# Order of the start-up and of the slots in a fused lightning-attention and mixture-of-experts kernel: x ahead of the decay rates, 12 of 16 decay tables and half of Wo in slot 0, counts behind the next q projection

## What is computed

```python
xn = layernorm(x)
# branch 1: lightning attention, 16 heads of 32, chunks of 128 tokens
q, k, v = silu(xn @ Wq), silu(xn @ Wk), silu(xn @ Wv)
D[c, s] = exp(ld * (c - s)) * (c >= s)                 # one table per head
o_intra = ((q @ k.T) * D) @ v
o_inter = (q @ S) * exp(ld * (c + 1))
S_new   = exp(ld * 128) * S + (k * exp(ld * (127 - s))).T @ v
gate    = (xn @ Wg1) @ Wg2
o       = rmsnorm_per_head(o * sigmoid(gate)) * norm_w
attn    = o @ Wo
# branch 2: 8 experts, top 2 of 8, capacity 1280 tokens per expert
moe     = sum over the kept top-2 of  p * (relu(xn @ w1[e]) @ w2[e])
out     = x + attn + moe
```

## Time and profile before

| | us |
|---|---|
| median of 3 runs | 2138.87 (2136.01 to 2139.21) |
| the profiled execution | 2135.27 |
| its span, first to last instruction | 2133.5 |
| PE busy | 2061.2 (97%) |
| DVE busy | 826.1 (39%) |
| ACT busy | 549.3 (26%) |
| POOL busy | 481.7 (23%) |
| mean granted TensorE clock | 0.991 of full speed |

### The profile page before, as it was taken

The page is one execution under the profiler, slowest core; times in us unless marked ns, Lnnn a source line. Parts: engine busy times, 40 slices in busy tenths (PEclk is TensorE's granted clock), DMA queues, the critical chain, the costliest instruction groups (busy, mean ns, idle before and its releaser), DMA issues.

```text
span 2133.5 us, 27452 instructions
## 1 busy us (share of the span) xinstructions
PE 2061.2 (97%) x11288; PEld 1691.5 (79%) x11288; DVE 826.1 (39%) x1582; ACT 549.3 (26%) x985; POOL 481.7 (23%) x371
## 2 busy tenths in 40 slices
PE   5899999999989999999999999999999999999997
PEld 3677787778778888888888888888888888888886
DVE  4666676667563123223312422321242124223211
ACT  4223222332232123212312312321231123123211
POOL 2544454435430202021120211102020102111011
PEclk9899999999999999999999999999999999999999
DMA  4320212012142214133321512422151215124021
GB/s 145 88 81 21 81 61 81 27 65 91 42 141 88 41 45 117 58 70 73 116 45 45 161 29 63 116 61 40 50 141 31 47 40 163 27 65 114 20 31 20
DMA packets 83961, 151.34 MB, mean 71 GB/s; under 512 B 16768, under 2 KB 16768, under 8 KB 83824
## 3 DMA queue, kind: packets, MB, share of 16 engines
q1 hardware_dynamic: 63424, 105.65, 14.9%
q0 software_dynamic: 20400, 43.74, 11.3%
HBM read 109.82 MB, written 39.53 MB: 70 GB/s over the span
## 4 chain that ended last, share of the span: by engine, by line
PE 88%; DVE 5%; DMA 2%; issue 2%; ACT 1%; POOL 1%; another core or an unknown queue 1%; SPq 0%; POOLq 0%; DVEq 0%; ACTq 0%
PE bank L1092 45%; PE bank L1359 32%; PE bank L1099 2%; PE bank L1215 2%; PE bank L1399 2%; PE bank L1182 1%; DVE xnT_lo L810 1%; PE bank L1141 1%; PE bank L1204 1%; PE bank L1198 1%; DVE turned L913 0%; DVE gated L911 0%; DVE stats L793 0%; ACT oT_hi L676 0%
## 5 line engine op out<-in xcount | busy, mean ns | idle before, releaser
L1044 DVE SCALAR_TENSOR_TENSOR h_lo<-bank,h_hi 128x512 fp32r<-128x512 f32 x256 | 176.9, 691 | 788.9 <-ACT h_hi L750 781.9
L1092 PE MATMUL bank<-xT_hi,w_hi 128*128 128x512 f32 x1024 | 406.6, 397 | 1.1 <-issue 1.0
L1359 PE MATMUL bank<-w_hi,h_hi 128*128 128x512 f32 x1024 | 398.6, 389 | 1.6 <-DVE h_lo L1044 1.6
L1092 PE MATMUL bank<-xT_hi,w_lo 128*128 128x512 f32 x1024 | 399.5, 390 | 0.0
L1359 PE MATMUL bank<-w_hi,h_lo 128*128 128x512 f32 x1024 | 398.7, 389 | 0.0
L1092 PE MATMUL bank<-xT_lo,w_hi 128*128 128x512 f32 x1024 | 398.5, 389 | 0.0
L1359 PE MATMUL bank<-w_lo,h_hi 128*128 128x512 f32 x1024 | 398.4, 389 | 0.0
L750 ACT ACTIVATE h_hi<-bank 128x512 fp32r<-128x512 f32 x256 | 153.1, 598 | 820.0 <-PE bank L1092 806.8
L577 POOL DMA_INDIRECT out_rows<-y,add_row x80 | 128.2, 1603 | 777.5 <-ACT y L743 706.7
L1359 PEld LDWEIGHTS bank<-w_hi,h_hi 128*128 128x128 f32 x1024 | 192.2, 188 | 42.4 <-DVE h_lo L1044 2.5
L1092 PEld LDWEIGHTS bank<-xT_hi,w_lo 128*128 128x128 f32 x1024 | 192.2, 188 | 41.7
(11 more groups left out here) (185 smaller groups left out, 2382.8 us busy)
## 6 DMA issues: line engine op xcount, KB each, us to landing
raw_weights<-in_L_ffn_w SPq DMA_DIRECT2D x256, 256.0 KB, 4.2
x_in<-in_L_attn_x SPq DMA_DIRECT2D x32, 256.0 KB, 3.1
xn_rows<-xn SPq DMA_DIRECT2D x32, 256.0 KB, 2.4
x_res<-in_L_attn_x SPq DMA_DIRECT2D x32, 256.0 KB, 4.4
out_rows<-y_attn SPq DMA_DIRECT2D x32, 256.0 KB
out_rows<-y,add_row POOLq DMA_INDIRECT x80, 6.0
gathered<-xn_rows,gather_row POOLq DMA_INDIRECT x76, 3.5
attn_raw<-in_L_attn_Wq SPq DMA_DIRECT2D x4, 256.0 KB, 8.0
```

Source lines behind the costliest of these rows:

```text
L1044: v_.scalar_tensor_tensor(h_lo[f % 2][:, 0:n * P], h_bank[f % 2][:, 0:n * P], 0.0, h_hi[f % 2][:, 0:n * P].bitcast(F32), ALU.max, ALU.subt ...
L1092: last = mm(dest, at(left[l], t), at_r(right[r], t), start=(i == 0), stop=(i == n - 1))
L1359: last = mm(y_bank[i][:, :], hx[f % 2][:, part], wx[c][:, f % FPC, :], start=(f == 0 and l == 0), stop=(f == FT - 1 and l == 2))
```

## The change

- SP loads tiles 0 to 3 of x first. The decay rates are started from ACT's own queue, as the first thing that ACT does.
- ACT makes 4 of the 16 decay tables at the start (those of unit 0) and 12 in slot 0, between tanh(0) and silu of q(1). The small high parts are made ahead of silu of q(0). The high part of Wo moves behind silu of k(1). In every unit the squares of unit u-1 are made right behind tanh(u), where those of unit u stood at the unit's end, and oT_hi(u-1) stands ahead of the four `xnT_high` in the third unit.
- POOL masks 4 tables at the start and 12 at the head of slot 0; `norm_scale(2)` moves from ahead of the slot table's initialisation to behind the 8 routes of slot 0.
- DVE makes `diff` ahead of the first `norm_pair`. The low part of Wo, `norm_pair(2)` and `normalise` of tiles 4 and 5 move from ahead of `choose(0)` into slot 0, behind `gate_output(0)`. In every unit all four masks go together, mean square of u-1 follows, then the states, `give_slots`, `scale_heads(u-1)` and oT_lo(u-1), and only then, in the third unit, the four xnT_lo. In a first unit one `add_residual` goes ahead of `norm_pair`.
- PE turns the router logits between v tiles 0 and 1, where it did so behind v tile 3, and counts behind the q projection of the next unit, where it did so behind `score`. At the end `project_out(2)` is split, and its third part waits for oT_lo behind `turn_first(3)`.

```diff
@@ -337,12 +337,4 @@
 
-            load_x(0)
-            load_x(1)
-            sp.dma_start(ld_row[:, :], log_decay.partition_broadcast(P)).then_inc(S["decays_loaded"], 16)
-            ld_groups = log_decay.rearrange("(g h) -> h g", h=HPG)
-            for h in range(HPG):
-                sp.dma_start(ld_col[h * HD:(h + 1) * HD, :],
-                             ld_groups[h, :].partition_broadcast(HD),
-                             allow_slow_non_contiguous=True).then_inc(S["decays_loaded"], 16)
-            load_x(2)
-            load_x(3)
+            for t in range(TPG):
+                load_x(t)
             for u in range(UNITS):
@@ -487,9 +479,12 @@
 
-            pool.wait_ge(S["tables_made"], HEADS)
-            g_.affine_select(out=intra_decay[:, :, :], in_=intra_decay[:, :, :],
-                             compare_op=ALU.is_ge, fill=0.0, base=0, pattern=[[0, HEADS], [1, P]],
-                             channel_multiplier=-1).then_inc(S["tables_masked"], 1)
+            def mask_tables(first, behind):
+
+                pool.wait_ge(S["tables_made"], behind)
+                g_.affine_select(out=intra_decay[:, first:behind, :], in_=intra_decay[:, first:behind, :],
+                                 compare_op=ALU.is_ge, fill=0.0, base=0, pattern=[[0, behind - first], [1, P]],
+                                 channel_multiplier=-1).then_inc(S["tables_masked"], 1)
+
+            mask_tables(0, HPG)
             decayed_k(0)
             decayed_q(0)
-            norm_scale(2)
 
@@ -539,2 +534,4 @@
                     head_scales(u - 1)
+                else:
+                    mask_tables(HPG, HEADS)
                 if i == 0:
@@ -550,2 +547,4 @@
                             route(g, t, r)
+                    if g == 0:
+                        norm_scale(2)
                     if g < SUPERS - 1:
@@ -612,2 +611,8 @@
             a = nc.scalar
+            act.dma_start(ld_row[:, :], log_decay.partition_broadcast(P)).then_inc(S["decays_loaded"], 16)
+            ld_groups = log_decay.rearrange("(g h) -> h g", h=HPG)
+            for h in range(HPG):
+                act.dma_start(ld_col[h * HD:(h + 1) * HD, :],
+                              ld_groups[h, :].partition_broadcast(HD),
+                              allow_slow_non_contiguous=True).then_inc(S["decays_loaded"], 16)
             act.wait_ge(S["decays_loaded"], 16 * (1 + HPG))
@@ -618,5 +623,9 @@
             a.activation(chunk_decay[:, :], ld_col[:, :], ACT.Exp, scale=float(P)).then_inc(S["decay_made"], 1)
-            act.wait_ge(S["diff_ready"], 1)
-            for h in range(HEADS):
-                a.activation(intra_decay[:, h, :], diff[:, :], ACT.Exp, scale=ld_row[:, h:h + 1]).then_inc(S["tables_made"], 1)
+
+            def decay_tables(heads):
+                act.wait_ge(S["diff_ready"], 1)
+                for h in heads:
+                    a.activation(intra_decay[:, h, :], diff[:, :], ACT.Exp, scale=ld_row[:, h:h + 1]).then_inc(S["tables_made"], 1)
+
+            decay_tables(range(HPG))
 
@@ -685,3 +694,2 @@
             weights_high("k")
-            silu_q(0)
             act.wait_ge(S["small_loaded"], 16 * 7)
@@ -689,2 +697,3 @@
             a.copy(g2_hi[:, :], g2_raw[:, :]).then_inc(S["small_hi"], 1)
+            silu_q(0)
             silu_k(0)
@@ -694,3 +703,2 @@
                 silu_v(t)
-            weights_high("o")
 
@@ -708,2 +716,6 @@
                 a.activation(tanh_g[:, :], proj[1][:, :], ACT.Tanh, scale=0.5).then_inc(S["tanh_ready"], 1)
+                if u > 0:
+                    square(u - 1)
+                if u == 0:
+                    decay_tables(range(HPG, HEADS))
                 if u < ATTN_UNITS - 1:
@@ -711,2 +723,6 @@
                     silu_k(u + 1)
+                if u == 0:
+                    weights_high("o")
+                if u > 0:
+                    oT_high(u - 1)
                 if i == 2 and g < SUPERS - 1:
@@ -714,6 +730,2 @@
                         xnT_high(TPG * (g + 1) + j)
-                if u > 0:
-                    oT_high(u - 1)
-                if u < ATTN_UNITS - 1:
-                    square(u)
                 if i == GROUPS - 1 and g < SUPERS - 1:
@@ -833,3 +845,3 @@
                 dve.wait_ge(S["scored"], u + 1)
-                dve.wait_ge(S["tables_masked"], 1)
+                dve.wait_ge(S["tables_masked"], 1 if u == 0 else 2)
                 for r in rs:
@@ -948,4 +960,2 @@
 
-            norm_pair(0)
-            norm_pair(1)
             dve.wait_ge(S["consts_made"], 3)
@@ -953,2 +963,4 @@
             v_.memset(taken[:, :], 0.0).then_inc(S["carry_zero"], 1)
+            norm_pair(0)
+            norm_pair(1)
             for t in range(TPG):
@@ -973,6 +985,2 @@
             gate_low(0)
-            weights_low("o")
-            norm_pair(2)
-            normalise(TPG)
-            normalise(TPG + 1)
 
@@ -983,8 +991,8 @@
                 g, i = u // GROUPS, u % GROUPS
-                mask(u, (0, 1))
-                if i == 0:
-                    read_counts(g)
+                mask(u, range(HPG))
                 if u > 0:
                     mean_square(u - 1)
-                mask(u, (2, 3))
+                if i == 0:
+                    read_counts(g)
+                states(u)
                 if i == 0:
@@ -995,6 +1003,2 @@
                         v_.tensor_scalar(spare_used[:, 1, :], taken[0:1, :], float(MAIN + P), None, ALU.is_gt).then_inc(S["spare_known"], 1)
-                states(u)
-                if i == 2 and g < SUPERS - 1:
-                    for j in range(TPG):
-                        xnT_low(TPG * (g + 1) + j)
                 if u > 0:
@@ -1002,8 +1006,19 @@
                     oT_low(u - 1)
+                if i == 2 and g < SUPERS - 1:
+                    for j in range(TPG):
+                        xnT_low(TPG * (g + 1) + j)
                 gate_output(u)
+                if u == 0:
+                    weights_low("o")
+                    norm_pair(2)
                 if i == 0:
+                    if g > 0:
+                        add_residual(TPG * (g - 1), proj[0])
                     if g < SUPERS - 1:
                         norm_pair(2 * (g + 1) + 1)
+                    if g == 0:
+                        normalise(TPG)
+                        normalise(TPG + 1)
                     if g > 0:
-                        for j in range(TPG):
+                        for j in range(1, TPG):
                             add_residual(TPG * (g - 1) + j, proj[j % 2])
@@ -1243,3 +1258,3 @@
             pe.wait_ge(S["g1_lo_made"], 1)
-            pe.wait_ge(S["logits_copied"], 1)
+            turn_logits(0)
             project_v(1)
@@ -1250,3 +1265,2 @@
             pe.wait_ge(S["consts_made"], 12)
-            turn_logits(0)
 
@@ -1255,4 +1269,2 @@
                 score(u)
-                if i == 0:
-                    count(g)
                 turn_kd(u)
@@ -1270,2 +1282,4 @@
                 project("q", u + 1, proj[0], "q_projected")
+                if i == 0:
+                    count(g)
                 update_states(u)
@@ -1294,3 +1308,3 @@
                     pe.wait_ge(S["g1_lo_made"], g + 2)
-                    pe.wait_ge(S["logits_copied"], g + 2)
+                    turn_logits(g + 1)
                     project_v(TPG * (g + 1) + 1)
@@ -1300,3 +1314,2 @@
                     project_v(TPG * (g + 1) + 3)
-                    turn_logits(g + 1)
 
@@ -1314,8 +1327,8 @@
             turn_first(1)
-            pe.wait_ge(S["oT_lo_made"], u)
-            project_out(2, last_out_bank[2], (0, 1, 2), True, False)
+            project_out(2, last_out_bank[2], (0, 1), True, False)
             turn_first(2)
             turn_first(3)
-            project_out(0, last_out_bank[0], (2,), False, False)
-            project_out(1, last_out_bank[1], (2,), False, False)
+            pe.wait_ge(S["oT_lo_made"], u)
+            for j in range(3):
+                project_out(j, last_out_bank[j], (2,), False, False)
             pe.wait_ge(S["gated_ready"], u + 1)
```

10 lines of the change are left out of this document (5 added, 5 removed).

## The result

| | before | changed |
|---|---|---|
| median of 15 runs, us | 2136.57 (2135.08 to 2143.05) | 2144.77 (2140.10 to 2147.87) |
| ratio to before, 95% interval | | 1.0028 (1.0019 to 1.0038) |
| profiled execution, span | 2133.5 | 2144.8 |
| PE busy | 2061.2 | 2071.7 |
| mean granted TensorE clock | 0.991 | 0.986 |

The account below looks back on a forecast made before the run. PE was taken as the bound, 88% of the chain, so only its waits could go. Terms summed to 20.95 us gained: 2135.3 to 2114.3 on the profile's scale, 2118 as a median, range 2109 to 2130.

Parts of the forecast that it names:

- Start-up: Before score(0): 12 fewer early tables give 3.5 us, earlier small parts 1.5, with the decays' landing taken as unchanged.
- Slots 0 and 1: From score(0), T, to attend(1): T+29.85 in place of T+38.0, a gain of 8.2 us, bounds 6 to 10.
- Groups: Groups 1 to 6: 13.8 us of waits go, 3.3 come at fourth scores, so 10.5 gained, bounds 4 to 13.8.
- oT_lo would end at about 240.4: Third unit of a group, DVE: second xnT_lo then ends at 241.7 to 242.1, so score(11) waits 0.3 to 0.8 us.
- the paragraph on the last units: Units 29 to 31: head_scale starts two masks, 1.2 us, later; three times on the path, taken as -2.8 us.
- In the groups the projections cover it: In the groups, head_scale starting 1.2 us later behind four masks was said to be hidden by the projections.
- In the groups POOL has ample time there: Against the rival that later routes delay kdT and nothing is gained, 2138.9 us, chance 0.04.
- The clock: In the slower rival, chance 0.04: TensorE falls to the lower of its clocks behind each wait at the fourth score.
- Group 0, fourth unit: Its kd wait goes, its score waits 2.1 us for xnT_lo: net -1.3 us, bounds -3 to 0.8.
- the one with the chance of 0.04: Slower: DVE's chain over 3 us longer, fourth-score waits above 3.8 us in seven groups; 2147.5 at 5 us each.
- The first rival: oT_lo and scaling meet POOL's work in every other group: fourth-score wait 3.1 us in three groups, 2125, chance 0.22.
- Group 7 and the last units: Group 7's count wait goes, a gain of 1.35 us; waits in the last units grow by 2.8.

Follow-up runs that it names:

- e1: The changed kernel with each unit's four masks in two pairs again and the mean square between them: 2111.16 us, 0.9863 of the kernel before.
- e4: The changed kernel with 14 extra matmuls filling TensorE's wait for xnT_lo at the fourth score: 2133.52 us, 0.9971 of the kernel before.
- e6: e1 with the three parts of project_out(2) together ahead of turn_first(2), as before the change: 2110.41 us, 0.9866 of the kernel before.
- e8: The changed kernel with POOL holding the next unit's kdT in third units until oT_lo is done: 2136.41 us, 0.9985 of the kernel before.

## Why the prediction was wrong

**Start-up: right.** q(0) was forecast near 19.4 and started at 19.08. The decays landed at 11.63, before at 11.73, though they were issued 0.9 us sooner, so the unknown landing was as taken. The Trainium skill, "DMA: Bandwidth & Descriptors", section "Issuing engines are not separate DMA queues", says that a second issuing engine saves only the time of the issue; this landing does not speak against it, but it is no clean test, since x went ahead of the decays in the same change. score(0) came at 42.36, 0.6 later than the sum's 41.7: wv_lo took 4.27 beside POOL, and v tile 0 waited 0.66 for it. The 0.3 for g1T_parts did not go either.

**Slots 0 and 1: right in kind, 1.3 too much.** attend(1) came at T+31.15 where T+29.85 was forecast. The first route began at T+10.6 and not 9.5: it waited for the slot numbers, which stand behind the states now, and of which one small operation took 1.31 beside POOL's mask. The waits of 4.4 and 6.5 forecast at turn_kd(1) and attend(1) were 5.7 and 4.6. ACT's timeline has both table loads of slot 0:

```profile
44.64 0.61 ACT L716 ACTIVATE tanh_g<-bank 128x512 f32<-128x512 f32 x1
45.27 1.28 ACT L628 ACT_TABLE_LOAD   x1
46.56 3.62 ACT L628 ACTIVATE intra_decay<-diff,ld_row 128x128 f32<-128x128 f32 x12
50.20 1.28 ACT L652 ACT_TABLE_LOAD   x1
51.50 0.60 ACT L652 ACTIVATE qT<-bank 128x512 f32<-128x512 f32 x1
```

Each load starts 0.02 behind the operation before it and is followed 0.01 to 0.02 later by the next. The Trainium skill, "ScalarE: Activation LUTs", section "What ACT_TABLE_LOAD costs", adds a drain of some 1.38 us to each switch; no such gap shows at either load, so here the measured 1.28 decides.

**Groups: the waits that go, right; the one that comes, wrong.** 13.8 us of waits went as forecast. The step that failed is the one that sets the new wait, "oT_lo would end at about 240.4", that is 10.8 behind the score. It took head_scale where it was before (4.32 behind the score), and scaling, oT_hi and oT_lo right behind it. But head_scale starts behind the mean square, and that now behind four masks. The prediction had this delay of 1.2, in the paragraph on the last units, and let it go with "In the groups the projections cover it". They don't, since it is a chain from unit to unit. From the masks of unit 13 to those of unit 14 it takes 9.6 with the masks in pairs (e1) and 11.2 in the changed kernel, and PE's unit is 10.0. What is over 10.0 is carried from the second unit to the third, and there the 1.2 comes again (head_scale at 6.76 for 4.32). Then the scaling falls on kdT and takes 1.05 more. The first xnT_lo starts 13.8 behind the score; with the masks in pairs it starts at 10.9, where the prediction had it. e1 shows this with one line: there the waits at the fourth score are 0.46 and 0.23, near the 0.8 and 0.3 of the forecast, and the profiled execution takes 2112.8, near the 2114.3 forecast on that scale.

"In the groups POOL has ample time there" failed too, though nothing of it shows in PE's waits. In group 3 rstd stands on POOL behind the eight routes and ahead of xn and the masks of unit 13. Before, it was done 2.1 ahead of score(13) at 290.02:

```profile
287.18 0.76 POOL L450 TENSOR_TENSOR rstd<-var_eps,minus_half 128x2 f32<-128x2 f32 x1
...
290.74 0.99 DVE L803 TENSOR_SCALAR xn<-x_in,moments,rstd 128x512 f32<-128x512 f32 x2
```

In the changed kernel it is done 1.3 behind score(13) at 287.55, and xn waits for it:

```profile
288.14 0.75 POOL L442 TENSOR_TENSOR rstd<-var_eps,minus_half 128x2 f32<-128x2 f32 x1
...
288.93 1.00 DVE L815 TENSOR_SCALAR xn<-x_in,moments,rstd 128x512 f32<-128x512 f32 x2 [0.57 <-issue]
```

It is so in all six middle groups. The slot numbers stand behind the states now and come 1.2 to 1.6 later in the first unit, which itself is 2.0 to 2.3 shorter, so the masks of the second unit start 2.3 to 2.7 behind its score where it was 1.63. e1 has the same late masks there and no long wait; what would come of moving rstd was not tried.

**The clock** was named in the rival only, and not in the sum. A wait of 3.4 costs 1.7 more by e4's ratio, 2.1 by its trace. The groups 1 to 6 add up in the traces: the first unit is 2.1 shorter (its waits make up 1.6 of this; the rest stands in no row of waits), some 0.7 of kd's waits goes, 3.4 for xnT_lo comes and 2.0 for the clock, together +2.6, and +2.65 was measured.

**Group 0, fourth unit.** A loss of 1.3 was forecast and 5.0 measured: -0.8 for kd, and the same wait of 3.4 with 2.6 for the clock, where 2.1 was taken for the wait.

**Rivals.** What came is the one with the chance of 0.04, by its mechanism (a chain some 3 us longer, 13.8 for 10.8; scaling held by POOL, and oT_lo a little, 0.99 for 0.69; the lower clock behind the waits) and nearly by its price: at 5 us each it gave 2147.5, and 3.4 with 1.7 to 2.1 is 5.1 to 5.5, at 2144.8. The first rival, that oT_lo and scaling fall on POOL's work in every other group, named one part of it; it came in all seven. "Nothing in the middle groups shows a chain so long" was said of the old order, and the chain had to be followed through the new one.

**Group 7 and the last units: the sum right, partly by luck.** Forecast +2.8 - 1.35 = +1.45, measured +1.6 from score(28) to the end. Group 7's first unit gave 1.47. But the waits grew by 0.8 only, where 2.8 was forecast: before they were 1.9 (kd), 0.5, 1.7 and 0.8, in the changed kernel 1.3 (attend(30)), 1.1, 0.2, 2.0 (attend(31)) and 1.0. The forecast left out that kd's 1.9 would go, and it left out the clock behind attend(31), which from its start to the next turn took 3.7 where it was 2.1:

```profile
609.89:612.89 3.00, 2.67 (x24) 2.43 (x28) 1.56 (x3) 0.00 (x0) 1.59 (x1) 0.56 0.08 30
```

The two nearly cancel. And with the masks in pairs (e1) the way from score(28) to the experts' first wait for h_lo is only 0.6 shorter than in the changed kernel (74.1 for 74.75; before 73.35), since xT_lo is waited for instead, 4.1 for 1.0; it takes e6's old end as well to bring it to 72.3. So the price of the four masks in the last units was over-rated.

## What to carry to other kernels

When an instruction is put ahead of one that feeds another engine, follow the chain through the other engines back to the same place in the next unit, and compare its length with the unit's: below it a delay is hidden, above it every unit adds to it. A reordering must be checked against what runs beside it in the new place, since a shift of one or two microseconds can bring two operations together that never met. A sum that comes out right is to be read term by term, since two terms that were left out can cancel. And a wait of TensorE of two or three microseconds is to be priced with the clock behind it, which for the waits of 3.4 was another 1.5 to 2.9 here.

## What the runs showed of the hardware

- Some operations on DVE take longer while POOL works on a tensor operation, even tiny ones. In the changed kernel var_eps, 128x2 elements, took 2.49 in slot 0 while POOL's kdT and qdT ran from 58.21 to 60.72, where it takes 0.17. DVE's timeline:

```profile
58.25 2.49 DVE L809 TENSOR_SCALAR var_eps<-moments 128x2 f32<-128x2 f32 x1
```

  The Trainium skill, "SBUF — State Buffer", section "Who interferes with whom", says that the two engines share a pair of ports; for operations of DVE with two SBUF inputs or in a 2-port mode the engine that issues first has the pair for its whole instruction, and the other blocks. The 0.69 and 1.75 of e8 agree: kdT had started 0.07 ahead of scaling. So does this row, but for one thing: var_eps was held through two operations of POOL, one right behind the other.
- Such a stop may travel further than its own length. In group 2 of the changed kernel var_eps took 1.30 beside qdT, the second residual sum came behind it, and the fourth sum, which shares its buffer, started at 214.58, though its product was there at 213.4. `project_gate` then waited for that sum, and unit 9 took 10.46 in place of 10.0. That the fourth sum waited for the second one's store follows from the program and is not shown by a releaser in the trace; in group 1 var_eps took 1.28 and the fourth sum was not late.
- Gaps of PE and the granted clock behind them: 0.76 and 1.93 (kd, before), 0.46 (e1) and 1.16 (e8, group 0) left it at 1.00. All gaps of 3.36 to 3.50 in the changed kernel took it to the 1.2 GHz level, and so did some that were shorter: 2.04 at attend(31) (0.56 from 609.89 to 612.89), and in e8 2.12 in group 1 (0.62 from 162 to 166), 2.07 in group 5 (0.57 from 448 to 452) and 2.45 in group 6 (0.57 from 520 to 524).
- The changed kernel's 15 runs spread over 7.8 us and those of the kernel before over 8.0, so the spread is not of the change's making. Those of e1 lie within 3.9, but they are four. What spreads the runs was not tried.
